# Cross attention and a 4-bit layer: first weight pieces, first context batch and the layer norm of x handled differently

## The reference, cut to what matters

```python
def xattn(text, features, Wq, bq, Wk, bk):        # text = layernorm(x), features = ctx, both (8, 256, 1024)
    Q = einsum('btx,dx->btd', text, Wq) + bq
    K = einsum('bpx,dx->bpd', features, Wk) + bk
    attn = softmax(einsum('btd,bpd->btp', Q, K) / 32, axis=-1)
    return einsum('btp,bpd->btd', attn, features)
def ffn(x, qweight, qzeros, scales, bias, g_idx): # 4-bit words of qweight, one scale and zero per group
    w = (qweight[:, None, :] >> shifts[None, :, None] & 15).reshape(-1, 1024)
    wbin = where(w > 0, 1.0, -1.0)
    return x @ (scales[g_idx] * (wbin - zeros[g_idx])) + bias
x = x + xattn(layernorm(x), ctx, Wq, bq, Wk, bk)
return x + ffn(layernorm(x), ...)
```

## Time and profile before

| what | value |
|---|---|
| median of 3 runs (lowest to highest) | 554.11 us (554.05 to 554.15) |
| the profiled execution: its own time, its span | 553.43 us, 551.6 us |
| PE (matmul) busy | 542.7 us, 98% |
| DVE, ACT, POOL busy | 385.6, 239.1, 184.5 us (70%, 43%, 33%) |
| mean granted TensorE clock | 1.000 |
| DMA moved, mean rate | 107.08 MB, 194 GB/s |

### The profile page before, as it was taken

The page is one execution under the profiler, slowest core; times in us unless marked ns, Lnnn a source line. Parts: engine busy times, 40 slices in busy tenths (PEclk is TensorE's granted clock), DMA queues, the critical chain, the costliest instruction groups (busy, mean ns, idle before and its releaser), DMA issues.

```text
span 551.6 us, 7449 instructions
## 1 busy us (share of the span) xinstructions
PE 542.7 (98%) x2702; PEld 454.9 (82%) x2702; DVE 385.6 (70%) x644; ACT 239.1 (43%) x426; POOL 184.5 (33%) x139
## 2 busy tenths in 40 slices
PE   8999999999999999999999999999999999999997
PEld 7888888887777767778889999998788888888886
DVE  4987776689889997894213555574777789778742
ACT  6964344411431341342427666676463253334210
POOL 1071000010000000000225977777667545743630
PEclk9999999999999999999999999999999999999999
DMA  8852100349677845744344799998427776774311
GB/s 291 289 167 64 38 1 0 116 159 315 213 204 260 227 191 177 224 165 158 116 159 185 259 358 351 318 402 328 198 81 241 214 230 228 229 228 126 106 76 76
DMA packets 47411, 107.08 MB, mean 194 GB/s; under 512 B 3632, under 2 KB 24184, under 8 KB 45200
## 3 DMA queue, kind: packets, MB, share of 16 engines
q1 hardware_dynamic: 40848, 100.33, 51.9%
q10 hardware_dynamic: 6528, 6.29, 5.4%
HBM read 66.70 MB, written 39.85 MB: 193 GB/s over the span
## 4 chain that ended last, share of the span: by engine, by line
PE 69%; DVE 15%; DMA 7%; ACT 5%; issue 3%; POOL 1%; ACTq 0%; SPq 0%; DVEq 0%; POOLq 0%
PE bank L1242 16%; PE bank L1244 16%; PE bank L1243 16%; PE bank L1286 5%; PE bank L1292 5%; PE bank L1289 5%; DMA xq<-xn_scratch 3%; PE bank L1346 2%; DVE xq L953 2%; DVE junk L1008 2%; DVE stats L918 2%; DMA right_scratch<-part_hi 2%; DVE xT_lo L859 2%; DVE part_t L1047 1%; DMA xn_scratch<-xin 1%
## 5 line engine op out<-in xcount | busy, mean ns | idle before, releaser
L1242 PE MATMUL bank<-xT_hi,m_hi 128*128 128x512 f32 x256 | 101.3, 396 | 1.6 <-DVE xT_lo L859 1.6
L1244 PE MATMUL bank<-xT_hi,m_lo 128*128 128x512 f32 x256 | 99.7, 390 | 0.0
L1243 PE MATMUL bank<-xT_lo,m_hi 128*128 128x512 f32 x256 | 99.7, 389 | 0.0
L751 ACT ACTIVATE t_pair<-bank,ucol 128x512 f32<-128x512 f32 x32 | 22.0, 686 | 100.4 <-PE bank L1244 100.4
L1194 DVE TENSOR_TENSOR xres<-xres,bank 128x512 f32<-128x512 f32 x56 | 38.2, 682 | 36.2 <-PE bank L1244 36.0
L550 POOL TENSOR_TENSOR tT_lo<-t_pair,tT_hi 128x1024 fp32r<-128x1024 f32 x16 | 38.1, 2399 | 73.7 <-ACT tT_hi L592 73.7
L1242 PEld LDWEIGHTS bank<-xT_hi,m_hi 128*128 128x128 f32 x256 | 48.0, 188 | 14.1 <-issue 2.5
L529 POOL TENSOR_TENSOR pairs<-mv,pairs 128x2 f32<-128x2 f32 x8 | 5.6, 695 | 161.0 <-DVE mv L927 161.0
L564 POOL TENSOR_TENSOR l_lo_s<-l_sum_s,l_hi_s 128x512 fp32r<-128x512 f32 x32 | 40.5, 1298 | 56.0 <-DVE l_sum_s L1135 56.0
L1244 PEld LDWEIGHTS bank<-xT_hi,m_lo 128*128 128x128 f32 x256 | 48.0, 188 | 10.2
L1243 PEld LDWEIGHTS bank<-xT_lo,m_hi 128*128 128x128 f32 x256 | 48.1, 188 | 9.9 <-issue 0.2
(11 more groups left out here) (145 smaller groups left out, 1244.0 us busy)
## 6 DMA issues: line engine op xcount, KB each, us to landing
cin<-in_ctx SPq DMA_DIRECT2D x8, 1024.0 KB, 5.7
xres<-in_x SPq DMA_DIRECT2D x8, 1024.0 KB, 11.5
out<-xres SPq DMA_DIRECT2D x15, 512.0 KB, 5.9
right_scratch<-part_hi SPq DMA_DIRECT2D x28, 256.0 KB, 2.2
xn_scratch<-xin SPq DMA_DIRECT2D x6, 1024.0 KB, 5.0
xq<-xn_scratch ACTq DMA_DIRECT2D x24, 256.0 KB, 5.7
r_tile<-right_scratch SPq DMA_DIRECT2D x6, 1024.0 KB, 12.0
yn_scratch<-yin SPq DMA_DIRECT2D x6, 1024.0 KB, 4.0
```

What stands on the lines that cost most here:

```text
L1242: pe.matmul(out_, a_hi, b_hi, start=start, stop=False, skip_group_check=True)
L1243: pe.matmul(out_, a_hi, b_lo, start=False, stop=False, skip_group_check=True)
L1244: return pe.matmul(out_, a_lo, b_hi, start=False, stop=stop, skip_group_check=True)
```

## The change

It has three parts.

1. **First pieces.** The first four row pieces of Wq's blocks 0 and 1 come as two and two; Wk's slices 1 and 2 are loaded, split and waited for by halves, as slice 0 was; bq and bk are loaded after slice 3, the second halves of Wq ahead of slice 4, and `times_bq(c - 3)` stands where `times_bq(c - 2)` stood.
2. **First batch of ctx.** It is loaded a second time, as `cq`, by four DMAs in runs of 32 floats, so that VectorE transposes it by 32x32 blocks (`c_blocks`) into the banks that TensorE's `c_tr(0, u)` wrote; these calls go. The rows of `cin[0]` come in the matching order, by four DMAs, when `c_blocks` is done with `cq`, which lies in the same place.
3. **Layer norm of batches 2 to 7.** `x_stats` and `x_apply` move from VectorE to ScalarE, with the same tables of n, ahead of the other steps of an n: a Copy pass with a summing output, the negated mean, a Square pass with that mean as bias and a summing output, and an Identity pass with scale and bias. Their junk output `xjunk` lies on `s3` and `zz`, the sources of `tab`. GpSimd forms variance, power and shift.

```diff
         nmean = at("nmean", 1.125, [P, QT], F32)
         shift = at("shift", 1.15625, [P, QT], F32)
+        xsum = at("xsum", 1.1875, [P, QT], F32)
+        xsquares = at("xsquares", 1.21875, [P, QT], F32)
...
         s3 = at("s3", 188.25, [P, D], BF16)
         zz = at("zz", 190.25, [P, D], BF16)
         junk = at("junk", 200.25, [P, HALF], F32)
+        xjunk = [at(f"xjunk{t}", 188.25 + 2 * t, [P, D], BF16) for t in range(QT)]
...
+            def first_wq(b, lo, hi, done):
+                sp.dma_start(wq_stage[b][:, lo:hi, :], wq_rows[:, lo:hi, b * P:(b + 1) * P]).then_inc(done, 16)
+
+            first_wq(0, 0, 2, s_wq00[0])
+            for c in range(3):
                 if c == 2:
-                    for r, row in enumerate((bq, bk)):
-                        sp.dma_start(bcols[:, r, :], row.rearrange("(p c) -> p c", c=NB)).then_inc(s_small, 16)
-                if c == 3:
                     for b in range(2):
-                        first_wq(b, 1, s_wql[b])
+                        first_wq(b, 2, KH, s_wq0[b])
+                for h, done in enumerate((s_wk0[c], s_wkl[c])):
+                    cols = slice(h * HALF, (h + 1) * HALF)
+                    sp.dma_start(wk_stage[c][:, cols], wk_rows[:, c, cols]).then_inc(done, 16)
+                if c == 0:
+                    first_wq(1, 0, 2, s_wq00[1])
+            for c in range(3, NB):
+                if c == 4:
+                    for b in range(2):
+                        first_wq(b, KH, NB, s_wql[b])
                 if c == NB - 1:
                     load_wq(2)
                 if c >= N_STAGE:
                     sp.wait_ge(s_wklo, c - N_STAGE + 1)
                     sp.wait_ge(s_wkbq, c - N_STAGE + 1)
                 sp.dma_start(wk_stage[c % N_STAGE], wk_rows[:, c, :]).then_inc(s_wkl[c % N_STAGE], 16)
+                if c == 3:
+                    for r, row in enumerate((bq, bk)):
+                        sp.dma_start(bcols[:, r, :], row.rearrange("(p c) -> p c", c=NB)).then_inc(s_small, 16)
             sp.wait_ge(s_const, 5)
...
             def load_ctx(b):
-                if b < 2:
-                    sp.wait_ge(s_xlo, NB * PAIRS)
-                    if b == 1:
-                        for name in R_SUM:
-                            sp.wait_ge(s_lst[name], 16 * KH)
+                if b == 0:
+                    sp.wait_ge(s_cb, 4)
+                elif b == 1:
+                    for name in R_SUM:
+                        sp.wait_ge(s_lst[name], 16 * KH)
                 elif b == 2:
                     sp.wait_ge(s_t, NB * PAIRS)
                 else:
                     sp.wait_ge(s_cnlo, 4 * (b - 2))
-                    sp.wait_ge(s_ctr, 4 * (b - 2))
-                sp.dma_start(cin[b % 3], ctx_rows[b]).then_inc(s_cl[b % 3], 16)
+                    wait(sp, s_ctr, 4 * (b - 3))
+                if b == 0:
+                    rows = ctx[0].rearrange("(j t m) f -> m j t f", t=QT, m=4)
+                    for m in range(4):
+                        sp.dma_start(cin[0][32 * m:32 * m + 32, :, :], rows[m]).then_inc(s_cl[0], 16)
+                else:
+                    sp.dma_start(cin[b % 3], ctx_rows[b]).then_inc(s_cl[b % 3], 16)
...
             for p in range(PAIRS):
                 for j in range(NB):
                     n = NB * p + j
                     if n == NB * (PAIRS - 1) + 1:
-                        load_ctx(0)
+                        sp.wait_ge(s_xlo, NB * PAIRS)
+                        pieces = ctx[0].rearrange("(j m) (k a i) -> a j (m k) i", m=NB, a=4, i=32)
+                        for a in range(4):
+                            sp.dma_start(cq[32 * a:32 * a + 32, :, :].rearrange("p m (k i) -> p (m k) i", i=32),
+                                         pieces[a]).then_inc(s_cql, 16)
...
                         load_raw(b)
+            load_ctx(0)
             load_ctx(1)
...
             def rsqrt(n):
-                pool.wait_ge(s_stat, n + 1)
-                if n < B:
+                if n < 2:
+                    pool.wait_ge(s_stat, n + 1)
+                elif n < B:
+                    pool.wait_ge(s_xsq, QT * (n - 1))
+                    pool.tensor_scalar(mv[:, :, 1], xsquares, 1.0 / D, EPS, ALU.mult, ALU.add).then_inc(s_xvar, 1)
+                    pool.wait_ge(s_xvar, n - 1)
+                else:
+                    pool.wait_ge(s_stat, n - B + 3)
+                if n < 2:
                     pool.tensor_tensor(rstd, mv[:, :, 1], power, ALU.pow).then_inc(s_rstd, 1)
                 else:
                     pool.tensor_tensor(rstd, mv[:, :, 1], power, ALU.pow).then_inc(s_rpow, 1)
-                    pool.wait_ge(s_rpow, n - B + 1)
+                    pool.wait_ge(s_rpow, n - 1)
                     pool.tensor_tensor(shift, nmean, rstd, ALU.mult).then_inc(s_rstd, 1)
...
+            first_split(0)
+            for c in range(3):
+                if c == 2:
+                    wq_split(0, 0)
+                    wq_split(1, 0)
+                for h in range(2):
+                    cols = slice(h * HALF, (h + 1) * HALF)
+                    act.wait_ge((s_wk0[c], s_wkl[c])[h], 16)
+                    copy(wk_hi[:, c, cols], wk_stage[c][:, cols]).then_inc(s_wkhi, 1)
+                if c == 0:
+                    first_split(1)
...
 
             def c_hi(b, u):
-                act.wait_ge(s_ctr, 4 * b + u + 1)
+                if b == 0:
+                    act.wait_ge(s_cb, u + 1)
+                else:
+                    act.wait_ge(s_ctr, 4 * (b - 1) + u + 1)
...
+            def x_stats(b):
+                act.wait_ge(s_xraw[b % 2], 16 * (b // 2))
+                if b == 2:
+                    act.wait_ge(s_placed, 16 * 8)
+                    act.wait_ge(s_rstd, 2)
+                for t in range(QT):
+                    act.activation(xjunk[t], raw_rows(b)[:, t, :], ACT.Copy, accum_out=xsum[:, t:t + 1]).then_inc(s_xsum, 1)
+                act.wait_ge(s_xsum, QT * (b - 1))
+                act.activation(nmean, xsum, ACT.Copy, scale=-1.0 / D).then_inc(s_xmean, 1)
+                act.wait_ge(s_xmean, b - 1)
+                for t in range(QT):
+                    act.activation(xjunk[t], raw_rows(b)[:, t, :], ACT.Square, bias=nmean[:, t:t + 1],
+                                   accum_out=xsquares[:, t:t + 1]).then_inc(s_xsq, 1)
+
+            def x_apply(b):
+                act.wait_ge(s_rstd, b + 1)
+                if b == 2:
+                    act.wait_ge(s_xtr, NB)
+                else:
+                    act.wait_ge(s_xst, 16 * (b - 2))
+                act.wait_ge(s_dot, b)
+                for t in range(QT):
+                    act.activation(by_quadrant(xin[:, 1, t, :]), raw_rows(b)[:, t, :].rearrange("q (k a i) -> q k a i", k=NB, a=4),
+                                   ACT.Identity, bias=shift[:, t:t + 1], scale=rstd[:, t:t + 1]).then_inc(s_xn, 1)
+
             act.wait_ge(s_cons, 2)
+            x_stats(2)
             for p in range(PAIRS):
                 for j in range(NB):
                     n = NB * p + j
+                    if n in X_STATS:
+                        x_stats(X_STATS[n])
+                    if n in X_APPLY:
+                        x_apply(X_APPLY[n])
...
             def c_blocks(u):
+                if u == 0:
+                    dve.wait_ge(s_cql, 64)
+                if u > 1:
+                    dve.wait_ge(s_clo, u - 1)
+                dve.transpose(c_bank(0, u)[:, :].rearrange("p (k m j) -> p m k j", k=2, m=NB),
+                              cq.rearrange("p m (k i) -> p m k i", i=32)[:, :, 2 * u:2 * u + 2, :]).then_inc(s_cb, 1)
...
                         right_sums(SUMS.index(n))
                     for k, i in LO_AT.get(n, ()):
                         right_lo(k, i)
-                    if n in X_STATS:
-                        x_stats(X_STATS[n])
-                    if n in X_APPLY:
-                        x_apply(X_APPLY[n])
                     if n in X_ROWS:
                         row_terms(X_ROWS[n])
                     if n in X_BLOCKS:
                         x_blocks(X_BLOCKS[n])
+                    if p == PAIRS - 1 and j == 5:
+                        c_blocks(0)
+                        c_blocks(1)
                     if p == PAIRS - 1 and j == 6:
                         c_lo(0, 0)
+                        c_blocks(2)
                         c_lo(0, 1)
+                        c_blocks(3)
...
+                if b == 0 and c > 2:
                     pe.wait_ge(s_wklo, c + 1)
                 for n in range(2):
+                    if b == 0 and c in (1, 2):
+                        pe.wait_ge((s_wklo0, s_wklo)[n], c + 1)
                     cols = slice(n * HALF, (n + 1) * HALF)
...
                 if u == 0:
-                    pe.wait_ge(s_cl[b % 3], 16 * (b // 3 + 1))
-                if b == 0:
-                    pe.wait_ge(s_xlo, NB * PAIRS)
-                    pe.wait_ge(s_w, 4 * KH)
-                    if u >= 2:
```

(77 more changed lines are left out.)

53 lines of the change are left out of this document (18 added, 35 removed).

## The result

The changed kernel takes **558.76 us** (median of 6 runs, 557.93 to 561.58), the kernel before 554.08 (6 runs, 553.87 to 554.29): a ratio of 1.009, 95% interval 1.007 to 1.011. It is slower by 4.7 us. The forecast was 561.2, in a range of 556.5 to 570.0; the figure is near that of the first rival (558.5), but that rival's own sum has another make-up, as the part on the prediction tells. The profiled execution took 557.93 us with a span of 556.1, so the span is 4.5 longer than the 551.6 of before.

What follows compares the result with a forecast made beforehand. TensorE, busy 542.7 of 551.6 us, was taken as the bound. Second gather later +8.7 (start's 0.9 included), VectorE relief -1.6, ctx 0: +7.1 on the median 554.11 gives 561.2 us, range 556.5 to 570.

Steps and rivals of the forecast that it cites:

- the first rival: Reload of batch 2 gets a full DMA share, lands by 141: 558.5 us, or 560.9 with low clock; chance 0.2.
- The bound: Whole kernel: TensorE works 542.7 of 551.6 us, so only its idle time and instruction count can change the end.
- the first stall: First table gather: TensorE there at 128.75 waits for the onehot, ready 135.6, since xn(3) is late: 6.8 us.
- The table load of the upper bound: ScalarE's statistics passes: a table load for the square, with passes of 1.25, would make the wait over 10 us.
- The third rival: ScalarE's passes come in time for the gather, xn(3) ready by 124.85: 549.8 us, or 551.7; chance 0.07.
- The second stall: Second table gather: late reload of batch 2 lands near 144.0, so TensorE waits from 147.05 to 149.8: 2.75 us.
- The clock: After the idling at the first gather, TensorE may run at its lower clock: up to 2.4 us, hidden in later waiting.
- What VectorE gives back: By n = 14 VectorE is some 7 us lighter, so the xT_lo wait goes: -1.6 us, bounds -1.6 and 0.
- The start: First Wk slices: halves make wk_lo of slice 1 come earlier, gaining 0.9 us, bounds 0 and 0.9.
- ctx: First ctx batch: 16 transposes less, -1.8 us, against a 2.0 us stall for batch 1: nets 0, bounds -1.8 and +2.5.
- cq: New load of 8192 packets of 128 B: 15 us, ending near 261, costing nothing; cover gone above about 17 us.
- the second rival: Small packets of cq take beyond some 17 us and hold up the stores behind them: 570 to 571 us; chance 0.2.

Runs made afterwards that it cites:

- experiment 4: The changed kernel with the junk output of the statistics passes of batches 2 to 4 in a spare place, so without the table wait: 549.38 us, ratio 0.9918.
- experiment 5: The changed kernel with row_terms(3) one n later, so that pick(0) no longer stands behind it on VectorE: 557.46 us, ratio 1.0065.
- experiment 6: The changed kernel with 52 unread identity transposes on TensorE ahead of the first gather: 557.57 us, ratio 1.007.
- experiment 1: The kernel before with only the smaller first pieces of Wk and Wq: 552.27 us, ratio 0.9969.
- experiment 2: The kernel before with only the first ctx batch transposed by VectorE's blocks: 553.70 us, ratio 0.9998.
- experiment 3: The kernel before with only the layer norm of batches 2 to 7 moved to ScalarE: 560.30 us, ratio 1.0114.
- 9: The kernel before with only the layer norm moved to ScalarE, its junk output in a spare place: 551.00 us, ratio 0.9964.
- 7: The changed kernel with the load of ctx batch 1 issued ahead of that of ctx batch 0: 557.15 us, ratio 1.0057.
- 8: The changed kernel with junk output in a spare place and ctx batch 1 loaded ahead of batch 0: 547.79 us, ratio 0.9888.

## Why the prediction was right or wrong

**The bound and the first stall: right.** TensorE stood at the first gather from 128.6 (forecast 128.75). ScalarE's first pass began at 113.35 (113.9), the statistics of batch 2 took 4.84 us to 118.19 (4.9), xn(2) was ready at 121.93 (122.5), xn(3) at 130.95 (131.7), and the onehot ended at 134.83 (135.6). The stall was 6.4 us (6.8). Passes of 1.05 and 1.15 with an accumulator read of 0.19 that overlaps the next pass: the 1.1 taken was the middle. The table load of the upper bound doesn't show: the first square pass starts at 115.81, 0.04 after the mean's end. The wait for all 8 table pieces was named as the new wait, and experiment 4 shows that it decides the sign. The third rival (faster, 549.8) asked for xn(3) by 124.85; experiment 4 gives 121.85 and 549.38.

**The second stall: wrong.** The step that failed is "ScalarE issues the reload of batch 2 only after it has evicted n = 2, at 132.3". The profile shows the issues at 128.59 to 130.44, beside the application of batch 3 and ahead of the eviction that stands before them in the program (130.86). That ScalarE's queue stands still for as long as it issues, as the part on the chip and the core has it, doesn't hold here either: the two application passes run from 128.59 to 130.95 with the issues beside them. Experiment 4 shows the same:

```profile
119.48 1.35 ACTq L777 DMA_DIRECT2D xq<-xn_scratch  x3
...
121.75 0.67 ACT L831 ACTIVATE t_pair<-bank,ucol 128x512 f32<-128x512 f32 x1
```

In both cases, going by the times, every wait that stands ahead of the issues in the program was over by then. Where the eviction itself waited for TensorE, the issues came after its start (118.87 and 120.18 in the kernel before, 128.85 and 129.36 in experiment 4). The issue at 120.18 in the earlier trace rows is such a case, and I took its order to hold always.

The reload then had 2.8 us ahead of the raw loads (131.39) and was there by 135.94, not 144.0, so the second gather found its weights ready. The outcome is that of the first rival, which I gave 0.2, but not for its reason: it had the reload issued at 132.3 and served at a full share. What spoke against such a share isn't refuted: in experiment 5 the last two issues were 1.4 us later and the transposes began 4.2 us later.

**The clock: right in size, wrong in place.** I had bounded it at 2.4 us and hidden it in the second stall. Without that stall it stood in the open, 2.34 us between the gathers. So the second gather moved by 7.7 and not 8.7. In experiment 6, without the low clock, 0.8 us (trace) to 1.2 us (medians) of the 2.34 reached the end.

**What VectorE gives back: too small.** Forecast -1.6, which was also the bound; the ledger has 2.8 us between the third and the fifth gather. The waits of xT_lo and wt fell by 2.3 (1.6 and 0.9 before, 0.2 after); 0.5 I can't place. I had left out wt, which is in the same list as xT_lo.

**The start: too small.** 0.9 was forecast and called the upper bound. By the first matmul of the t stage it is 1.16 (101.92 before, 100.76 after) and 0.97 in experiment 1, whose medians say 1.7. I had read the wait for wk_lo from one execution, and the other traces without part 1 have longer ones.

**ctx: right.** The part nets nothing (-0.1 in experiment 2, forecast 0), for the reason given: the load of batch 1 stands behind that of batch 0, which waits for c_blocks. The stall was 1.2 us instead of 2.0, since VectorE's block transposes into the banks took 0.71 us and not 1.15. From the end of c_blocks(3) at 283.24 to the transposes of batch 1 at 293.1 it took 9.9 us, where the forecast has 9.7 (5.4 + 2.5 + 1.8; the 1.8 for first byte and landing stands in no row). The price of the block transposes:

```profile
L1135 DVE STREAM_TRANSPOSE bank<-cq 128x512 f32<-128x512 f32 x4 | 2.8, 712 | 0.1
```

**cq: the second rival falls.** Two views of the changed kernel, first SyncE's timeline with the issue, then one stretch of 2 us while the packets move:

```profile
248.97 6.05 SPq L459 DMA_DIRECT2D cq<-in_ctx  x4
```

```profile
254.00:256.00 2.00, 2.00 (x11) 1.65 (x10) 1.90 (x4) 0.00 (x0) 0.00 (x0) 1.00 0.89 141
```

8192 packets moved between 250 and 258 us, 1 MB at 125 to 142 GB/s, where I had taken 15 us. At 141 GB/s that is 1100 packets of 128 B per us, against the 545 of 512 B of Wq: the small packet costs half as much time, and not the same. Its stores in SyncE's queue came in time (257.77 us), and no wait for them or for cq is in TensorE's list. The Trainium skill, "DMA: Bandwidth & Descriptors", Specifications, states that line rate needs at least 512 B and that a smaller transfer is done as a read-modify-write. The rate did fall below 512 B, to 142 GB/s at most against 279, though 279 is itself below the 416 of a 1 MB load into 128 partitions. A doubled cost per packet, which I had thought possible by the second, doesn't show.

By sizes: 8.7 became 7.7, -1.6 became -2.8, 0 became -0.3; 7.1 became 4.5. That the first rival's 558.5 lies so near 558.76 is luck. With the low clock, which came, that rival said 560.9, and VectorE's larger gift took it down again. My own 561.2 is in part luck too: it holds a second stall of 2.75 us that didn't come, and 2.34 us of low clock came in its place.

## What to carry to other kernels

When work moves to another engine, list every semaphore that its first instruction there waits for, scratch outputs included. Here an output that nobody reads lay on the source of a late DMA and cost 8 us (experiment 3 against 9), while the move by itself gains 2. When a wait is cut, ask who stands next (experiment 5), and when a DMA is put behind a dependent one in a queue, try the other order first (experiments 7 and 8: 1.6 us for one swapped line).

## What the runs showed of the hardware

- ScalarE's DMA issues can run ahead of its arithmetic: issued at 128.59 to 130.44 in the changed kernel and from 119.48 in experiment 4, though evictions that start at 130.86 and 121.75 stand before them in the program. Where the eviction waited for TensorE (128.85 in experiment 4), the issue came behind its start (129.36). A reload's start can't be read from the end of the instruction in front of it.
- After TensorE had been idle from 128.6, the granted clock fell to 0.50 between 133 and 134. It was at 0.96 in the stretch from 140 to 141, after TensorE had worked from 134.98 on; the matmuls came every 0.43 us until then and every 0.23 from 140.25. Identity transposes in the gap kept it at 1.00.
- 128 B packets, four DMAs into 32 partitions each, moved at up to 142 GB/s, 1100 per us, where 512 B ones had moved at 545 per us.
- A 128x512 block transpose by VectorE took 0.71 us from cq and 1.15 us from yq in the same kernel; why they differ was not tried.
